# A residual chain on one core: b2 moves into the closing rank product, u is summed from both halves of C, and two PSUM copies go to ScalarE

## The reference

```python
def reference(x, condB_coeff, condB_codebook, itok_B_0_23, itok_B_4_50, mask, W0, b0, W1, scale_log, lora_A, lora_B, W2, b2, As, Bs, A3, B3):
    # layer 0: x W0' + b0 + coeff * (x (2 mask - 1))
    x = x + (einsum('bsi,oi->bso', x, W0) + b0) + einsum('bsi,bio->bso', x, 2 * mask - 1) * coeff[:, None, None]
    # layer 1: weights (W1 + lora_B lora_A / 2) quantised to a codebook of 8 levels per group, plus the delta
    x = x + x @ w_eff.T
    # layer 2: W2, its bias b2, and a rank-16 pair picked by itok_B_0_23
    x = x + einsum('bti,oi->bto', x, W2) + b2 + einsum('btr,bro->bto', einsum('bti,bir->btr', x, As[tok]), Bs[tok]) * 2
    # layer 3: a rank-16 pair picked by itok_B_4_50
    x = x + einsum('bnr,bor->bno', einsum('bni,bri->bnr', x, B3[tok3]), A3[tok3])
    return x
```

## Time and profile before

| | |
|---|---|
| device time, median of 3 runs | 550.66 us (550.19 to 551.02) |
| the profiled execution: its own time | 549.87 us |
| its span | 548.2 us |
| PE busy | 533.4 us (97%) |
| DVE busy | 468.8 us (86%) |
| ACT busy | 341.7 us (62%) |
| POOL busy | 192.9 us (35%) |
| granted TensorE clock | 1.0 throughout |

### The profile page before, as it was taken

How to read it: one execution, slowest core, us unless ns; L and a number is a source line. 1 busy time by engine, 2 the same in 40 slices (tenths; PEclk the granted TensorE clock), 3 DMA queues, 4 the chain that set the end, 5 groups by cost and what they waited for, 6 DMA issues and landing times.

```text
span 548.2 us, 8917 instructions
## 1 busy us (share of the span) xinstructions
PE 533.4 (97%) x2856; PEld 454.1 (83%) x2856; DVE 468.8 (86%) x723; ACT 341.7 (62%) x658; POOL 192.9 (35%) x179
## 2 busy tenths in 40 slices
PE   5999999999999999999999999999999999999997
PEld 4988888888888787887888788788888878878886
DVE  5998898988865879977999989998997998999862
ACT  3777776776745874586566657557566665755720
POOL 2669867987734020012034204111410420411130
PEclk9999999999999999999999999999999999999999
DMA  8766041843486995558456545645835654664122
GB/s 232 244 92 148 21 125 48 248 138 115 102 186 189 348 326 100 189 157 171 138 161 167 123 160 175 114 155 189 172 134 168 167 126 158 180 103 168 61 59 77
DMA packets 145261, 84.06 MB, mean 153 GB/s; under 512 B 102672, under 2 KB 118032, under 8 KB 145104
## 3 DMA queue, kind: packets, MB, share of 16 engines
q1 hardware_dynamic: 143312, 78.97, 52.4%
q0 software_dynamic: 1632, 4.72, 3.4%
...
## 4 chain that ended last, share of the span: by engine, by line
PE 83%; DVE 9%; ACT 4%; DMA 3%; issue 1%; POOL 0%; DVEq 0%; ACTq 0%; SPq 0%; POOLq 0%
PE bank L1637 19%; PE bank L1644 10%; PE bank L1676 7%; PE bank L1677 7%; PE bank L1675 7%; PE bank L1511 5%; PE bank L1513 5%; PE bank L1512 5%; PE bank L1726 3%; PE bank L1725 3%; PE bank L1727 3%; PE bank L1691 3%; PE bank L1421 2%; PE bank L1704 1%; DVE w_lo L1074 1%; DVE merged_ring L1168 1%
## 5 line engine op out<-in xcount | busy, mean ns | idle before, releaser
L1637 PE MATMUL bank<-x_t_pair,m_hi 128*128 128x512 f32 x512 | 128.5, 393 | 1.5 <-ACT m_hi L800 1.4
L800 ACT CAST m_hi<-merged_ring 128x512 fp32r<-128x512 f32 x128 | 73.1, 619 | 60.7 <-PE bank L1644 31.9
L1637 PEld LDWEIGHTS bank<-x_t_pair,m_hi 128*128 128x128 f32 x512 | 92.5, 189 | 19.2 <-ACT m_hi L800 2.3
L1174 DVE TENSOR_TENSOR m_lo<-merged_ring,m_hi 128x512 fp32r<-128x512 f32 x128 | 86.3, 720 | 12.5 <-ACT m_hi L800 12.2
L576 POOL TENSOR_TENSOR x_t_pair<-x_sum,x_t_pair 128x256 fp32r<-128x256 f32 x32 | 29.7, 960 | 179.1 <-ACT x_t_pair L861 179.1
L1168 DVE TENSOR_TENSOR merged_ring<-merged_ring,w_t 128x1024 f32<-128x1024 f32 x64 | 82.1, 1311 | 11.3 <-ACT merged_ring L790 10.3
L790 ACT ACTIVATE merged_ring<-mask_ring,batch_now 128x1024 f32<-128x1024 int32 x64 | 78.0, 1241 | 21.1 <-DMA mask_ring<-in_mask_Bx4096x_ik 20.3
L1644 PEld LDWEIGHTS bank<-x_t_pair,m_lo 128*128 128x128 f32 x512 | 69.8, 190 | 5.0
L1644 PE MATMUL bank<-x_t_pair,m_lo 128*128 128x256 f32 x512 | 71.4, 282 | 0.0
L1676 PE MATMUL bank<-P_lo,x_t_pair 128*128 128x512 f32 x160 | 62.3, 389 | 0.0
L1675 PE MATMUL bank<-P_hi,x_t_pair 128*128 128x512 f32 x160 | 62.3, 389 | 0.0
...
## 6 DMA issues: line engine op xcount, KB each, us to landing
mask_ring<-in_mask_Bx4096x_ik SPq DMA_DIRECT2D x64, 512.0 KB, 4.4
...
```

The source lines that it names most:

```text
L800: nc.scalar.copy(Mh[:, n % MR], ring_f[:, k % MR, h * HALF:(h + 1) * HALF]).then_inc(s["h_set"], 1)
L1174: nc.vector.tensor_tensor(Ml[:, n % MR], ring_f[:, k % MR, h * HALF:(h + 1) * HALF], Mh[:, n % MR].bitcast(F32), ALU.subtract).then_inc(s[ ...
L1637: mm(bank[L0_BANK[HT * h + j]][:, :], Mh[:, n % MR, j * P:(j + 1) * P], xThl[:, :, :, k + i, :], start=(k + i == 0), stop=False, skip_grou ...
```

## The change

b2 is split once, early, into a high part (ACT) and a low part (POOL); SP stores both as two rows in DRAM (`b2_dram`). Each batch's table `Gs` gets these two rows as its rows 96 and 97, in place of the 32 rows that belonged to the sum from C's low part, and `Us` has constant ones there (a memset, once). The closing product then has 98 rows of depth. The sum from C's low part is added to u itself: after ACT's evacuation (now 32 rows) DVE does three additions of 32 rows instead of one of 64, and one copy into `Us` instead of two. All additions of b2 by DVE and POOL go, and with them the row tile and its load. ScalarE now copies the first output block out of PSUM (`out_copy`, behind the four `x_hi` casts of the next batch, and after the last batch), and in batches 2 to 7 the first product's snapshot (`c11_set`, behind the last `x1_hi`); DVE did both with an addition.

The diff, cut to its changed lines (renamed semaphores left out):

```diff
@@ -67,6 +67,7 @@
+    b2_dram = nc.dram_tensor("b2_dram", [2, D], F32, kind="Internal").ap()
@@ -161,7 +162,6 @@
-    b2all = at("b2_rows", [P, D], F32, reg_b2)
@@ -190,6 +190,8 @@
+    b2h = const("b2_hi", [P, KT], F32R)
+    b2l = const("b2_lo", [P, KT], F32R)
@@ -230,6 +232,8 @@
+        G_ROWS = ((0, 0), (0, 32), (1, 64))
+        U_ROWS = 98
@@ -386,6 +390,9 @@
+            sp.wait_ge(s["b2_split"], 2)
+            for part, v in enumerate((b2h, b2l)):
+                sp.dma_start(b2_dram[part].rearrange("(t p) -> p t", p=P), v[:, :].bitcast(F32), allow_slow_non_contiguous=True).then_inc(s["b2_stored"], 16)
@@ -413,7 +420,10 @@
-                sp.wait_ge(s["out_added"], 4 * b + i + 1)
+                if i:
+                    sp.wait_ge(s["out_added"], 3 * b + i)
+                else:
+                    sp.wait_ge(s["out_copied"], b + 1)
@@ -443,15 +453,15 @@
-                for part, rows in ((0, 0), (0, 32), (1, 64), (0, 96)):
+                for part, rows in G_ROWS:
...
+                sp.wait_ge(s["b2_stored"], 32)
+                sp.dma_start(Gs0[96:U_ROWS, :].bitcast(F32), b2_dram).then_inc(s["g_in"], 16)
...
-                sp.wait_ge(s["xt_later"], 2)
-                sp.dma_start(b2all[:, :], row(b2).broadcast_to([P, D])).then_inc(s["b2row_in"], 16)
@@ -553,6 +563,8 @@
+            pool.wait_ge(s["b2_split"], 1)
+            nc.gpsimd.tensor_tensor(b2l[:, :], b2c[:, :], b2h[:, :].bitcast(F32), ALU.subtract).then_inc(s["b2_split"], 1)
@@ -564,9 +576,10 @@
-                for part, rows in ((0, 0), (0, 32), (1, 64), (0, 96)):
+                for part, rows in G_ROWS:
...
+                nc.gpsimd.dma_start(Gs[96:U_ROWS, :].bitcast(F32), b2_dram).then_inc(s["gl_in"], 16)
@@ -588,24 +601,11 @@
-            def v_bias(b):
-                pool.wait_ge(s["c_sums"], 4 * (b - 1))
-                nc.gpsimd.tensor_tensor(vsum[:, :], vsum[:, :], b2all[:, HALF:D], ALU.add).then_inc(s["v_biased"], 1)
...
-            def p_bias(b):
-                pool.wait_ge(s["out_added"], 4 * b + 2)
-                nc.gpsimd.tensor_tensor(c_sum[:, :], c_sum[:, :], b2all[:, HALF:D], ALU.add).then_inc(s["p_biased"], 1)
...
-            pool.wait_ge(s["out_added"], 8)
-            nc.gpsimd.tensor_tensor(b2all[:, HALF:D], b2all[:, HALF:D], b2all[:, 0:HALF], ALU.subtract).then_inc(s["b2_diff"], 1)
-            pool.wait_ge(s["b2_diff"], 1)
...
-                v_bias(b)
-                p_bias(b)
@@ -696,6 +696,7 @@
+                    nc.scalar.copy(b2h[:, :], b2c[:, :]).then_inc(s["b2_split"], 1)
@@ -821,6 +822,18 @@
+            def c11_set(b):
...
+                act.wait_ge(s["prod_done"], 4 * (b - 1) - 3)
+                act.wait_ge(out_stored[2], 16 * b)
+                nc.scalar.copy(c_sum[:, :], bank[MAIN_BANK[0]][:, :]).then_inc(s["c11_set"], 1)
...
+            def out_copy(b):
+                act.wait_ge(s["out_done"], 4 * b + 1)
+                if not isinstance(b, int) or b:
+                    act.wait_ge(out_stored[0], 16 * b)
+                nc.scalar.copy(OUT_PLACE[0], bank[MAIN_BANK[0]][:, :]).then_inc(s["out_copied"], 1)
@@ -865,6 +878,7 @@
+                    out_copy(0 if second else b - 1)
@@ -894,15 +908,16 @@
+                if not first and not second:
+                    c11_set(b)
...
-                both = slice(0, 64)
-                nc.scalar.activation(usum[both, :], bank[RANK_BANK][both, T:2 * T], ACT.Identity, bias=now[both, 2:3]).then_inc(s["u_part"], 1)
-                act.wait_ge(s["u_summed"], b + 1)
+                nc.scalar.activation(usum[0:32, :], bank[RANK_BANK][0:32, T:2 * T], ACT.Identity, bias=now[0:32, 2:3]).then_inc(s["u_part"], 1)
+                act.wait_ge(s["u_summed"], 3 * (b + 1))
@@ -914,6 +929,7 @@
+            out_copy(NB - 1)
@@ -1154,6 +1170,7 @@
+            nc.vector.memset(Us[96:128, :].bitcast(F32), 1.0).then_inc(s["ones_set"], 1)
@@ -1208,21 +1225,16 @@
-                if first and i == 0:
-                    dve.wait_ge(s["b2row_in"], 16)
...
-                h = OUT[i][1]
-                added = b2all[:, h * HALF:(h + 1) * HALF]
-                if not plain and i == 2:
-                    dve.wait_ge(s["p_biased"], b - 1)
-                if not plain and i == 3:
-                    dve.wait_ge(s["v_biased"], b - 1)
-                if not plain and i:
-                    added = vsum[:, :] if i == 3 else c_sum[:, :]
-                nc.vector.tensor_tensor(OUT_PLACE[i], bank[MAIN_BANK[i]][:, :], added, ALU.add).then_inc(s["out_added"], 1)
+                o = bank[MAIN_BANK[i]][:, :]
+                if plain:
+                    ins = nc.vector.tensor_copy(OUT_PLACE[i], o)
+                else:
+                    ins = nc.vector.tensor_tensor(OUT_PLACE[i], o, vsum[:, :] if i == 3 else c_sum[:, :], ALU.add)
+                ins.then_inc(s["out_added"], 1)
@@ -1282,22 +1294,19 @@
-            def c11_seen(b):
...
-                dve.wait_ge(s["prod_done"], 4 * (b - 1) - 3)
-                dve.wait_ge(out_stored[2], 16 * b)
-                nc.vector.tensor_tensor(c_sum[:, :], bank[MAIN_BANK[0]][:, :], b2all[:, 0:HALF], ALU.add).then_inc(s["c_sums"], 1)
+            def c_sum_up(b):
...
-                dve.wait_ge(s["c_sums"], 4 * (b - 1) - 3)
+                dve.wait_ge(s["c11_set"], b - 1)
...
-                dve.wait_ge(s["c_sums"], 4 * (b - 1) - 2)
+                dve.wait_ge(s["c_sums"], 3 * (b - 1) - 2)
...
-                dve.wait_ge(s["c_sums"], 4 * (b - 1) - 1)
+                dve.wait_ge(s["c_sums"], 3 * (b - 1) - 1)
@@ -1315,8 +1324,7 @@
-                    for i in range(2):
-                        out_add(b - 1, i, old, second)
+                    out_add(b - 1, 1, old, second)
@@ -1357,7 +1365,7 @@
-                    c11_seen(b)
+                    c_sum_up(b)
@@ -1373,11 +1381,12 @@
-                both = slice(0, 64)
-                nc.vector.tensor_tensor(usum[both, :], usum[both, :], bank[RANK_BANK][both, 0:T], ALU.add).then_inc(s["u_summed"], 1)
-                dve.wait_ge(s["u_summed"], b + 1)
+                for n, (rows, cols) in enumerate(((0, 0), (32, 0), (32, T))):
+                    if n:
+                        dve.wait_ge(s["u_summed"], 3 * b + n)
+                    nc.vector.tensor_tensor(usum[0:32, :], usum[0:32, :], bank[RANK_BANK][rows:rows + 32, cols:cols + T], ALU.add).then_inc(s["u_summed"], 1)
+                dve.wait_ge(s["u_summed"], 3 * (b + 1))
...
-                nc.vector.tensor_copy(Us[96:128, :], usum[32:64, :]).then_inc(s["u_ready"], 1)
@@ -1658,9 +1667,11 @@
-                elif o in (0, 2, 3, 4):
...
-                    pe.wait_ge(s["out_added"], 4 * (b - 1) + max(o, 1))
+                elif o == 0:
+                    pe.wait_ge(s["out_copied"], b)
+                elif o in (2, 3, 4):
...
+                    pe.wait_ge(s["out_added"], 3 * (b - 1) + o - 1)
@@ -1694,14 +1705,15 @@
+                    pe.wait_ge(s["ones_set"], 1)
...
-                pe.wait_ge(s["u_ready"], 3 * (b + 1))
+                pe.wait_ge(s["u_ready"], 2 * (b + 1))
...
-                    ins = mm(bank[MAIN_BANK[i]][:, :], Us[:, t * P:(t + 1) * P], table[:, h * HALF:(h + 1) * HALF],
+                    ins = mm(bank[MAIN_BANK[i]][:, :], Us[0:U_ROWS, t * P:(t + 1) * P], table[0:U_ROWS, h * HALF:(h + 1) * HALF],
@@ -1753,19 +1765,19 @@
-                pe.wait_ge(s["c_sums"], 4 * (b - 1) - 3)
+                pe.wait_ge(s["c11_set"], b - 1)
...
-                pe.wait_ge(s["c_sums"], 4 * (b - 1) - 1)
+                pe.wait_ge(s["c_sums"], 3 * (b - 1) - 1)
...
-                pe.wait_ge(s["c_sums"], 4 * (b - 1))
+                pe.wait_ge(s["c_sums"], 3 * (b - 1))
...
```

6 lines of the change are left out of this document (3 added, 3 removed).

## The result

The changed kernel takes 557.34 us (median of 4, 556.66 to 558.18) against 550.42 us of the kernel before (4 runs, 550.10 to 551.02): a ratio of 1.0127, 95% interval 1.0112 to 1.0142. It is 6.9 us slower. The forecast was 551.5 us in a range of 550.3 to 553.0, so it was wrong. The profiled execution took 556.66 us with a span of 555.0 us, 6.8 us over the 548.2 of before.

A forecast was written before the change was run, and what follows sets the result against it. The prediction took PE's own matmul pitch as the bound. On the profiled execution 549.87 + 0.72 (u chain) + 0.10 (preamble cast) = 550.69 us; the median stands 0.79 us higher, so 551.5 us, range 550.3 to 553.0.

The forecast's parts named there:

- The two stores of b2: SP's stores ahead of batch 0's x: 2048 pieces occupy 16 DMA engines 1.1 us, covered by ACT's idle time; cost 0.
- rival 1: Slower: the small stores hold the queue 14.4 us, delaying x, W0's last part and first masks; about 563 us, chance 0.07.
- The slack behind the stores: ACT's 2.09 us of idle time ahead of its first cast of x, taken to cover delay from the stores.
- The u chain, batch 0: DVE's longer sums for u delay PE's first closing product: +0.72 us, between +0.48 and +0.84.
- Rival 4: PE's wait at batch 0's close is not for u, or DVE arrives sooner: no cost there, 550.8 us, chance 0.13.
- The u chain, other batches: The chain grows 0.7 us but stays under 1.9 us of cover ahead of PE's close; no cost.
- The closing depth: 32 closing matmuls with 98 instead of 128 rows: taken as 0, at most 2.9 us.
- Rival 2: Slower: pipe restart at each closing matmul, +2.9 us (554.4), or at each closing, 0.7 us (552.2); chance 0.08.
- The copies on ACT, and what goes: ACT's snapshot and block copies fit idle time, cost 0; removed DVE and POOL additions and bias load gain 0.
- Rival 3: Slower: ACT's copies uncovered in some batches, `m_hi` late for layer 0: up to 4.0 us, about 553 to 555.5; chance 0.07.
- The preamble's cast: ACT's cast of b2 ahead of a quantiser step on the chain into PE: +0.10 us, between 0 and 0.20.
- the first paragraph of the prediction: From batch 1 to the last block the time is PE's own; savings on other engines cannot shorten it.

The follow-up runs named there:

- before_stores1: Kernel before plus b2's split and only the high part's store, 1024 pieces of 4 bytes, read by nobody: 555.64 us, ratio 1.0090.
- after_actq: Changed kernel with the two stores of b2 issued by ACT's DMA queue instead of SP's: 556.75 us, ratio 1.0115.
- after_rows: Changed kernel with b2 in another layout, each store 16 pieces of 256 bytes instead of 1024 of 4 bytes: 552.09 us, ratio 1.0033.
- rows_u_first: after_rows with DVE's five steps for u in batch 0 moved ahead of `t2_part`: 550.48 us, ratio 1.0006.
- rows_dve_copies: after_rows with the first out block and the first product's snapshot copied by DVE again, not ACT: 551.40 us, ratio 1.0024.
- rows_u_first_128: rows_u_first with closing products 128 rows deep instead of 98, b2's parts repeated 16 times against 1/16: 550.20 us, ratio 1.0014.

## Why the prediction was wrong

**The two stores of b2: the step that failed.** The prediction took them as 0, and they cost 5.7 us of layer 0's start. It read the share of 0.07 behind `y_dram` as what the store occupied: 9 ns a piece, 1.1 us for 2048. That much was right, the pieces pass at this rate (share 0.54 in 146 to 148). But it is the time in which the engines handle the pieces, not the time until they have landed, and transfers behind stand for most of that: 8.1 us here. The row could not have shown a hold, since nothing was queued behind `y_dram`; the next DMA on SP comes 9.4 us later:

```profile
66.14 0.34 SPq L372 DMA_DIRECT2D y_dram<-y_col  x1
75.54 0.33 SPq L328 DMA_DIRECT2D w0t_dram<-w_out  x1
```

The row that had it was the other one: the landing of 7.2 us for `y_dram`, a store of 128 pieces of 4 bytes that lie side by side, 16 in each 64 bytes, as here. The prediction took that as latency. It even had the rival (1, chance 0.07) with this mechanism, a hold of what stands behind. Its price of 563 us summed two landings, 14.4 us; the two stores hold for 8.1 us together, and one alone holds for 8.4 (`before_stores1`). The rival said that the queue is held; `after_actq` shows that it is more than the queue. It was wrong, too, to treat the long landing and the low share as two opinions on one quantity: they are both right, on different ones. The Trainium skill ("DMA: Bandwidth & Descriptors", Specifications) says that the DMA does a read-modify-write below 512 bytes. That was evidence on the right side, and was given too little weight. No run here shows whether it is the mechanism, and the threshold does not price it: behind pieces of 256 and of 32 bytes the x loads' issue is within 0.2 us of before, and pieces of 4 bytes cost by how close they lie.

**The slack behind the stores** was looked for on the wrong path. The prediction and its rival 1 took the 2.09 us of ACT ahead of its first cast of x. They were used up: the first signs start 7.4 us later (171.26 for 163.90), and the cast follows them without a gap. But ACT then idles 2.93 us more for `merged`. What decides is SP's path of the chain above. The last store of W0 is issued 6.3 us later (166.27 for 160.00). The mask behind it waits for its landing and is 7.3 us later (171.90 for 164.56). SP's own wait ahead of `w_t`, 165.45 to 168.42 before, takes 2.9 us of that, the longer landing of `w_t` adds 2.0, and PE had 0.7 to spare: 7.3 - 2.9 + 2.0 - 0.7 = 5.7 us. That the hold less ACT's slack, 8.1 - 2.1 = 6.0, comes near the 5.7 is luck.

**The u chain, batch 0.** +0.72 forecast, +0.77 in the changed kernel, 0.75 when taken away, 0.69 by the gap at the close. Right, step by step: three dependent sums, one cast, one subtraction.

```profile
219.84 1.26 DVE L1387 TENSOR_TENSOR u_sum<-u_sum,bank 32x256 f32<-32x256 f32 x3
221.14 0.28 DVE L1389 CAST u_batch<-u_sum 32x256 fp32r<-32x256 f32 x1
221.58 0.41 DVE L1391 TENSOR_TENSOR u_batch<-u_sum,u_batch 32x256 fp32r<-32x256 f32 x1 [0.15 <-ACT u_batch L921]
```

221.58 - 219.84 = 1.74 us from the first sum to the subtraction; the prediction had 1.76. Rival 4 falls.

**The u chain, other batches**: no wait of PE ahead of L1716 in them. Right.

**The closing depth**: taken as 0, measured 0.04 us a batch, 0.3 in all, well inside its bound of 2.9; the groups of four take 1.09 us and not the 1.07 that were foreseen. Rival 2 falls in both forms, 2.9 and 0.7.

**The copies on ACT, and what goes**: taken as 0, and no cost shows in the traces. Rival 3, up to 4.0 us, falls. DVE's and POOL's saved 45 us are beside PE's work.

**The preamble's cast**: +0.10 forecast. In the four kernels that have it without a hold (`after_rows`, `rows_u_first`, `rows_dve_copies`, `rows_u_first_128`) layer 0 starts between 174.91 and 175.45, on both sides of the 175.12 of before; so small a term can't be read from it, and it was not isolated.

With the stores repaired, the change measures near the forecast of 551.5: `after_rows` 552.09 (551.49 profiled), `rows_dve_copies` 551.40. As a difference it does so less well, since the kernel before took 550.22 beside them: 1.9 and 1.2 us more than before, where 0.8 was forecast. With the u steps moved ahead, and the depth back at 128, the change is level with the kernel before and not ahead of it: PE sets the time, as the first paragraph of the prediction had it, and what is taken off other engines comes back as nothing.
